# A four-layer graph attention network on one core: ring units made a step ahead, a slot's scores issued before its ring step

## What is computed

```python
# layers 0, 1 (one head):   e = leaky(s_src[i] + s_dst[j]);  attn = softmax(where(adj > 0, e, -9e15));  out = elu(attn @ h)
# layer 2 (eight heads):    e = leaky(q_i . k_j / 8 + edge_bias[adj]);  attn as above;  out = concat(attn @ v) @ Wp + bp
# layer 3 (additive, GATv2):
u = jnp.einsum('bnf,of->bno', hp, W1)
v = jnp.einsum('bnf,of->bno', hp, W2)
s = u[:, :, None, :] + v[:, None, :, :]
s = jnp.where(s > 0, s, ALPHA * s)
e = jnp.einsum('bijf,f->bij', s, a[:, 0])
e = jnp.where(adj > 0, e, NEG_INF)
attention = jax.nn.softmax(e, axis=2)
h_prime = jnp.einsum('bij,bjf->bif', attention, hp)
```

## Time and profile before

| | |
|---|---|
| median of two runs | 10125.54 us (10098.96 to 10152.13) |
| the profiled execution | 10139.95 us, span 10138.2 us |
| TensorE matmul busy | 8219.1 us, 81% |
| VectorE busy | 7548.4 us, 74% |
| ScalarE busy | 7262.9 us, 72% |
| GpSimd busy | 1505.4 us, 15% |
| DMA | 864.97 MB, mean 85 GB/s |
| mean granted TensorE clock | 0.944 |

### The profile page before, as it was taken

One profiled execution on the slowest core, in us unless ns is written; L12 is line 12 of the kernel. 1 busy time (PEld: TensorE's weight loads), 2 busy tenths in 40 slices (PEclk: granted clock), 3 DMA queues, 4 the chain that ended last, 5 costly groups with the idle time before them and its releaser, 6 DMA issues.

```text
span 10138.2 us, 176152 instructions
## 1 busy us (share of the span) xinstructions
PE 8219.1 (81%) x64968; PEld 3720.2 (37%) x64968; DVE 7548.4 (74%) x11028; ACT 7262.9 (72%) x8496; POOL 1505.4 (15%) x582
## 2 busy tenths in 40 slices
PE   5787878878788787888878878787887878878788
PEld 3434333343333434334343333433334333343332
DVE  5676867768677686777867777687786877767778
ACT  3576867767677686776867767677676776767778
POOL 0302103021030210302103030030300203012000
PEclk8899999999999999999999999999999999999999
DMA  4434233342433524334243342433424234242330
GB/s 100 120 69 114 70 88 87 70 113 68 94 88 72 118 55 98 89 71 114 55 105 82 76 113 51 106 82 82 106 59 111 71 90 98 63 107 69 89 81 20
DMA packets 519920, 864.97 MB, mean 85 GB/s; under 512 B 91938, under 2 KB 157474, under 8 KB 518946
## 3 DMA queue, kind: packets, MB, share of 16 engines
q1 hardware_dynamic: 518946, 852.41, 36.2%
HBM read 76.25 MB, written 4.19 MB: 8 GB/s over the span
## 4 chain that ended last, share of the span: by engine, by line
PE 45%; DVE 20%; issue 14%; ACT 10%; DMA 7%; SPq 4%; DVEq 1%; ACTq 0%; POOL 0%; POOLq 0%
PE psum L876 23%; DVE work L1459 11%; DMA work<-work 7%; PE psum L747 6%; ACT work L1123 5%; PE psum L785 4%; PE psum L743 4%; SPq L537 3%; ACT work L981 3%; DVE work L1269 2%; PE psum L766 2%; ACT work L990 2%; PE psum L678 2%; DVE work L1297 1%; PE psum L673 1%
## 5 line engine op out<-in xcount | busy, mean ns | idle before, releaser
L876 PE MATMUL psum<-work,pick 128*32 128x512 f32 x32768 | 4162.3, 636 | 1528.6 <-DVE work L1459 989.6
L1123 ACT ACTIVATE work<-v,ucol 128x1024 f32<-128x1024 f32 x3582 | 3878.5, 1139 | 284.6 <-PE psum L876 283.4
L1459 DVE TENSOR_SCALAR work<-v,ucol 128x1024 f32<-128x1024 f32 x4610 | 3400.6, 792 | 311.5 <-PE psum L876 242.6
L876 PEld LDWEIGHTS psum<-work,pick 128*32 128x32 f32 x32768 | 1007.9, 113 | 3761.7 <-issue 2835.5
L1269 DVE CUSTOM_DVE_ANT_0 work<-psum,work 128x1024 f32<-128x1024 f32 x1280 | 1543.4, 1206 | 1067.8 <-ACT work L981 1065.9
L981 ACT ACTIVATE work<-psum,beta 128x1024 f32<-128x1024 f32 x1024 | 1135.6, 1109 | 1661.9 <-PE psum L747 1576.8
L1297 DVE STREAM_TRANSPOSE work<-work 128x1024 f32<-128x1024 f32 x1280 | 1583.9, 1237 | 769.2 <-DMA work<-work 768.5
L990 ACT ACTIVATE work<-work,least 128x1024 f32<-128x1024 f32 x1280 | 1459.8, 1140 | 26.4 <-DVE least L1269 26.3
L785 PE MATMUL psum<-work,vw 128*64 128x128 f32 x16384 | 1151.2, 284 | 21.2 <-DMA work<-work 21.1
L785 PEld LDWEIGHTS psum<-work,vw 128*64 128x64 f32 x16384 | 903.4, 140 | 510.7 <-issue 478.5
L743 PE MATMUL psum<-mask_next,ident_b 128*128 128x512 bf16 x2560 | 822.2, 405 | 222.1 <-DVE least L1269 115.5
(11 more groups left out here) (158 smaller groups left out, 5097.1 us busy)
## 6 DMA issues: line engine op xcount, KB each, us to landing
work<-work SPq DMA_DIRECT2D x2560, 256.0 KB, 4.6
adj_in<-in_adj SPq DMA_DIRECT2D x128, 512.0 KB, 5.0
tile3T<-blocks SPq DMA_DIRECT2D x512, 128.0 KB, 2.7
mask<-mask_next SPq DMA_DIRECT2D x128, 256.0 KB, 2.7
x_in<-in_x SPq DMA_DIRECT2D x16, 256.0 KB, 4.5
xT_both<-in_xT SPq DMA_DIRECT2D x16, 256.0 KB, 5.5
out<-yout SPq DMA_DIRECT2D x16, 256.0 KB, 2.7
work<-in_WqT SPq DMA_DIRECT2D x1, 128.0 KB
```

Of the source, the lines that this page charges most:

```text
L876: mm = pe.matmul(score3[32 * q:32 * q + 32, cols], pick[:, 15 - kk:47 - kk], ring[u % RING][q][:, cols], start=(kk == 0), stop=(kk == 15), ...
L1123: ins = act.activation(ring[u % RING][q], v3[:], ACT.Relu, bias=ucol[:, 4 * T + q, kk:kk + 1])
L1459: ins = dve.tensor_scalar(ring[u % RING][q], v3[:], ucol[:, 4 * T + q, kk:kk + 1], 0.0, ALU.add, ALU.max)
```

## The change

It has three parts. (1) On ScalarE and VectorE `ring_units` is called in slot s for the step after that slot's step (`STEPS[s] + 1`), and for step 0 once ahead of slot 0, behind `side_copies`. The last step's units are so made in the slot of the step before it. (2) On TensorE `scores` leaves `ahead` and is called first in the slot, ahead of the ring step; `uses_of` follows, so that a tile takes its PSUM buffer before `pv3`, `column3`, `values3` and `out3` of the same slot. (3) `shared_units` plans the split with the new times: over a body with both parts ScalarE gets 228 units in place of 225 and VectorE 284 in place of 287. No instruction is added or removed beyond that, no buffer and no DMA changes, and SyncE's and GpSimd's programs stay as they are.

```diff
@@ uses_of
         T, kk = of_step(s)
+        if ahead and s in TILE_AT:
+            uses.append(("a", TILE_AT[s]))
         if ring:
...
         if ahead:
-            if s in TILE_AT:
-                uses.append(("a", TILE_AT[s]))
@@ shared_units
-        if STEPS[s] is not None:
-            u = STEPS[s]
+        for u in ([0] if s == 0 else []) + ([STEPS[s] + 1] if STEPS[s] is not None and STEPS[s] + 1 < GROUPS else []):
             by_act, by_dve = max(act_at, ends[u]), max(dve_at, ends[u])
             n = min((1, 2, 3), key=lambda k: max(by_act + k * ACT_UNIT, by_dve + (4 - k) * DVE_UNIT))
             act_at, dve_at = by_act + n * ACT_UNIT, by_dve + (4 - n) * DVE_UNIT
-            pe_at = max(pe_at, act_at, dve_at) + PE_STEP
+            made.append(max(act_at, dve_at))
+            counts.append(n)
+        if STEPS[s] is not None:
+            pe_at = max(pe_at, made[STEPS[s]]) + PE_STEP
             ends.append(pe_at)
-            counts.append(n)
@@ TensorE: ahead
-                if s in TILE_AT:
-                    scores(a, it, TILE_AT[s])
@@ TensorE: layer3
                     T, kk = of_step(s)
+                    if more and s in TILE_AT:
+                        scores(g + 1, it, TILE_AT[s])
                     if kk is not None:
                         ring_step(g, 16 * T + kk)
@@ TensorE: the ahead part alone
             for s in range(SLOTS):
+                if s in TILE_AT:
+                    scores(0, first, TILE_AT[s])
                 ahead(0, first, s)
@@ ScalarE: layer3
                 side_copies(g, it)
+                ring_units(g, 0, more)
                 for s in range(SLOTS):
...
-                    if kk is not None:
-                        ring_units(g, 16 * T + kk, more)
+                    if kk is not None and STEPS[s] + 1 < GROUPS:
+                        ring_units(g, STEPS[s] + 1, more)
@@ VectorE: slots
                     if g is not None and kk is not None:
-                        ring_units(g, 16 * T + kk, a is not None)
+                        if STEPS[s] + 1 < GROUPS:
+                            ring_units(g, STEPS[s] + 1, a is not None)
                         last_top(g, s, tail)
```

More of the change, by code:

```diff
@@ L265, in shared_units @@
     act_at = dve_at = pe_at = 0.0
-    ends, counts = [0.0] * RING, []
+    ends, made, counts = [0.0] * RING, [], []
     for s in range(SLOTS):
```

## The result

The changed kernel took 9564.64 us (9553.52 to 9575.75, two runs) against 10125.54 before: a ratio of 0.945, 95% interval 0.933 to 0.956. Run again beside seven runs of the kernel before it gave 0.943 (0.941 to 0.946). The forecast was 9620 us with a range of 9280 to 9910. The profiled execution's span is 9551.7 us, 586.5 us less than before.

A forecast was written before the change was run, and what follows sets the result against it. No engine fills the span; engines waiting for each other in circles, mostly in layer 2, set the time. Gains 28 + 5 + 4 less 3 make 34 us a body, 510 us over 15 bodies: 9620 us, range 9280 to 9910.

The forecast's parts named there:

- two circles: Layer 2's waiting loops, by the DMA (18.3 us, four slots) and by ScalarE (7.8 us, two slots); gain 28 us.
- Circle A: Layer 2, four slots: product, DMA landing, transpose, leaky, units, ring step, scores, products; 18.3 us falling to 16.5 us.
- the sum: A body's gains less cost: 28 + 5 + 4 - 3 = 34 us of 626.2.
- The count of nine rounds: Of layer 2's 16 four-slot rounds, nine run by way of the DMA and seven by ScalarE.
- The cover of 0.26 us: Layer 2: VectorE's 4.2 us between two slots' leaky fits behind TensorE's 4.46 us of scores, ring step and half product.
- The PSUM order: Layer 2 scores wait for leaky instead of ScalarE's copy of the ring product; 5 us of 6 gained.
- Layers 0 and 1: Tile slots there, with VectorE and ScalarE nearly full: at most 5.7 us gained, 4 us taken.
- The read of a ring tile: Dense slots: VectorE's read of a finished tile now stands behind units; costs 3 us a body, at most 10.
- Rival 1: Layer 2: TensorE's gaps get too short for the clock to fall; 55 us a body, 9300 us; chance 0.16.
- Rival 2: VectorE's order or a later landing replaces the waits for units; 9 us a body, 10000 us; chance 0.15.
- Rival 3: TensorE's ring step is held by waiting scores; 24 us more a body, 10500 us; chance 0.05.

The follow-up runs named there:

- ring first: Changed kernel with TensorE's ring step put back ahead of the scores, the tile still taking its PSUM buffer first: 9407.79 us (ratio 0.927).
- units only: Kernel before with only the units made a step ahead, in the changed kernel's split; TensorE's order and PSUM uses as before: 9457.1 us (ratio 0.933).
- order only: Kernel before with only TensorE's scores ahead of the ring step and the PSUM uses that follow: 9524.18 us (ratio 0.939).
- reading first: Changed kernel with VectorE reading a finished ring tile ahead of that slot's units: 9446.76 us (ratio 0.931).

## Why the prediction was right, point by point

- **Layer 2 by two circles.** The mechanism holds. Circle A appears in the changed kernel's chain in the predicted order, with no units in it and the ring step between scores and product:

```profile
4232.39 1.05 PE psum L786 x16
4233.44 0.02 issue
...
4235.98 5.84 DMA work<-work
4241.82 0.02 issue
...
4243.01 1.19 DVE work L1273
...
4244.22 0.05 issue
4244.27 1.04 PE psum L744 x2
4245.31 1.71 PE psum L748 x4
4247.01 3.10 PE psum L875 x16
4250.11 1.02 PE psum L786 x16
4251.13 0.54 PE psum L744 x2
4251.67 0.92 PE psum L748 x4
4252.59 1.05 PE psum L786 x16
```

  That is 20.2 us; with the landing at 7.1 us rather than 8.4 and TensorE at full clock (scores 1.5, ring step 1.92) it is the 16.5 us of the sum. The size was off: 41 us of layer 2 against 28 + 5. What was mis-sized is the slots without a product, 66 to 76: they won 14.4 us and were not looked at apart; at the sum's 1.6 us per four slots they had 4 us. The other slots won 26.6 us, near the 29 us that this leaves for them. The count of nine rounds of circle A holds (8.0 times a body the chain passes the DMA before, 9.0 in the changed kernel), and it mattered little, as a round of either circle was put at nearly the same gain, 1.83 or 1.6 us.
- **The cover of 0.26 us.** It held in the changed kernel in 70 of 126 rounds, where the scores follow the first leaky, and failed where I built on it: in the kernel with the ring step first the VectorE branch is the circle.
- **The PSUM order.** The waits for ScalarE's copy went, as said. 3.3 us a body in place of 5, by ring first against units only.
- **Layers 0 and 1.** 4 us expected, 9.0 us came in slots 6 to 66 (7.4 in the second profile). The bound of 5.7 us was taken from the busy time of the tile slots only; units only and order only reach 7.5 and 8.7 us in the same slots. What gave it between the tile slots was not tested apart.
- **The read of a ring tile.** 3 us a body was too little for the dense slots: the waits there grew by 8.0 us, of which reading first returns 6.3 us; and 11.6 us came once in the last ring, where I had written that nothing waits. The bound of 10 us a body holds. Of 9.6 us given back at both ends of a body, reading first returns 3.0. The rest (6.6 us) is there in each kernel with units ahead (4.1 to 7.1 us beyond the kernel before) and mostly not in order only (1.2 us), so it comes with making units ahead of other work of the slot; by which instruction was not settled.
- **A wait not foreseen.** The scores of a head pair's first slots wait for `q_lo`, 185 us over the span. It stands behind the next step's units on VectorE, and scores first puts the ring step behind it too. With ring first it is 86 us.
- **Rival 1** (gaps and half clock go) did not happen in the changed kernel: the clock rose from 0.944 to 0.952 over the span and from 0.93 to 0.95 in layer 2, short of the 0.98 named, and the round above ran scores and ring step at half after its wait for the DMA. That agrees with the Trainium skill, page "TensorE: Matmul & The Clock Gate", section "HAM oscillation — how this bites in real kernels", where waits for a DMA between bursts of matmuls bring the half clock back. A good part of the half clock did go with the ring step first (27.0 to 12.9 us a body). **Rival 2** (VectorE's order, the DMA's landing) did not cancel the gain; the landing is still in nine rounds of the chain a body. **Rival 3** was half true: the ring step held by the scores costs 157 us against ring first. That is 10 us a body, far from the 34 us at which it would have decided.
- **The signs named beforehand.** Body 592 us: 586. Layer-2 stretch 312 us: 302. Waits before the ring step for units in the layer-2 window under 15 us: 0.3 us in one body, 2.8 us in the mean of all, 239 us over the whole span. DMA waits of VectorE about the same: 768.5 to 780.8 us. Scores waiting for leaky: 116 to 599 us.

So the mechanism was right, and that the time came within 1% of the forecast is in part luck, for the errors partly cancelled: a body's gain was put 13 us too low in layer 2 and in slots 6 to 66, its cost 7 us too low, and the last ring's 13.5 us were left out.

## What to carry to other kernels

Follow one round of the circle over all engines and add it up; then any of its members that can be made earlier, or that stands in it only by program order, gives its own length once, as long as no other branch is then the longest. Two edits that break the same circle need not add: try each alone, since the second may bring only its cost (here 46 and 113 us). When a round gets shorter, look at the granted clock too before the gain is divided by the number of rounds: here both moved. And when work is made ahead, look at what now stands behind it in the same program: a short instruction for which the busiest engine waits (here a 1.2 us read, worth 118 us) is worth trying in front.

## What was not expected of the hardware

36 matmuls a body more, with results that nobody reads, took 96 us off the kernel before: there TensorE at 1.2 GHz took 3.5 us for a ring step that takes 1.92 us at 2.4 GHz, after waits of 3.3 us between bursts, and its matmuls lay on the circle. A transfer of 256 KB landed in 4.7 us and one of 128 KB in 2.7 us; the DMA engines moved 91 GB/s in the mean of the changed kernel and were busy for 0.48 of its layer-2 window, yet halving the bytes of these moves made the kernels 3.4 to 4.6% faster.
